# Attention with a quaternion map on one core: the program rewritten in steps of two heads, with row-tiled score pairs

## The reference

```
qkv  = x @ Wqkv.T + bqkv
attn = softmax(q @ k.T / 4)                     # per head, 512 x 512
coh  = sigmoid(tanh([x, cond] @ Wc1.T + bc1) @ Wc2.T + bc2)
mod  = attn * coh;  mod = mod / (mod.sum(-1) + 1e-8)
fa   = softmax(fp(cond) @ pe.T)                 # one row of 512 per sequence
out  = ((1 - 0.21) * mod + 0.21 * fa) @ v
x1   = x + out @ Wout.T + bout
y    = x1 + rotate(filter(x1))                  # one fixed linear map of the features
```

## Time and profile before

| | us |
|---|---|
| time, median of 3 runs | 379.8 |
| lowest and highest run | 374.76, 381.87 |
| span of the profiled execution, first to last instruction | 375.9 |
| TensorE busy | 321.0 (85%) |
| TensorE weight loads busy | 189.0 (50%) |
| VectorE busy | 223.9 (60%) |
| ScalarE busy | 176.9 (47%) |
| GpSimd busy | 156.8 (42%) |
| mean granted TensorE clock | 0.904 of 2.4 GHz |

### The profile page before, as it was taken

One profiled execution on the slowest core, in us unless ns is written; L12 is line 12 of the kernel. 1 busy time (PEld: TensorE's weight loads), 2 busy tenths in 40 slices (PEclk: granted clock), 3 DMA queues, 4 the chain that ended last, 5 costly groups with the idle time before them and its releaser, 6 DMA issues.

```text
span 375.9 us, 5338 instructions
## 1 busy us (share of the span) xinstructions
PE 321.0 (85%) x1537; PEld 189.0 (50%) x1537; DVE 223.9 (60%) x385; ACT 176.9 (47%) x323; POOL 156.8 (42%) x129
## 2 busy tenths in 40 slices
PE   0848849999799889999799689999799779999975
PEld 0634426555456456655456356655456346544423
DVE  3765943786568616687577407686577517775102
ACT  2101103765356625556456415565356525667750
POOL 9979950099991000299400000199500030296000
PEclk9986975999989958999899958999899969999996
DMA  8698498214953992216924991125943990200001
GB/s 245 247 125 99 146 127 123 83 58 99 125 59 112 126 163 51 75 66 127 124 30 145 149 118 36 62 78 112 118 51 122 124 146 1 84 1 2 1 1 57
DMA packets 16518, 35.87 MB, mean 95 GB/s; under 512 B 2724, under 2 KB 8228, under 8 KB 14456
## 3 DMA queue, kind: packets, MB, share of 16 engines
q1 hardware_dynamic: 14968, 34.47, 50.4%
q10 hardware_dynamic: 1536, 1.23, 1.2%
HBM read 25.07 MB, written 10.50 MB: 95 GB/s over the span
## 4 chain that ended last, share of the span: by engine, by line
PE 63%; DMA 24%; DVE 4%; ACT 3%; issue 3%; SPq 1%; ACTq 0%; DVEq 0%
PE smax_ps L996 14%; PE st_ps L1018 14%; PE o_ps L1030 13%; DMA stack<-max_rows 10%; DMA stack<-qk_scratch 10%; PE job_ps L894 9%; PE job_ps L929 3%; PE job_ps L970 3%; ACT probs L594 2%; DMA qk_scratch<-qk_lo 2%; PE job_ps L951 2%; DVE qk_lo L672 2%; PE smax_ps L982 2%; DMA w_raw<-wqkvT 1%; DVE maxima L746 1%
## 5 line engine op out<-in xcount | busy, mean ns | idle before, releaser
L746 DVE TENSOR_REDUCE maxima<-smax_ps 128x1 f32<-128x512 f32 x256 | 168.3, 686 | 113.6 <-PE smax_ps L996 113.0
L594 ACT ACTIVATE probs<-st_ps 128x512 f32<-128x512 f32 x247 | 142.6, 597 | 137.0 <-PE st_ps L1018 135.6
L996 PE MATMUL smax_ps<-stack 127*128 127x512 f32 x256 | 118.0, 464 | 13.8 <-DMA stack<-qk_scratch 11.9
L1018 PE MATMUL st_ps<-stack 128*128 128x512 f32 x247 | 107.7, 439 | 19.8 <-DMA stack<-max_rows 18.2
L996 PEld LDWEIGHTS smax_ps<-stack 127*128 127x128 f32 x256 | 52.0, 204 | 51.5 <-DVE maxima L746 24.4
L1030 PE MATMUL o_ps<-probs,vals 128*32 128x512 f32 x512 | 71.7, 634 | 1.0 <-ACT probs L594 0.9
L1018 PEld LDWEIGHTS st_ps<-stack 128*128 128x128 f32 x247 | 50.5, 205 | 39.6 <-DMA stack<-max_rows 19.8
L419 POOL TENSOR_TENSOR vals<-v_new,vals 128x256 f32<-128x256 f32 x16 | 10.0, 641 | 94.5 <-PE o_ps L1030 94.5
L401 POOL TENSOR_TENSOR x_lo<-x_raw,x_hi 128x1024 fp32r<-128x1024 f32 x3 | 7.2, 2388 | 65.7 <-ACT x_hi L550 65.7
L894 PE MATMUL job_ps<-x_hi,w_hi 128*128 128x512 f32 x48 | 22.0, 459 | 10.0 <-DVE w_lo L797 9.5
L519 POOL TENSOR_TENSOR prod<-amap,x_tok 128x1024 f32<-128x1024 f32 x12 | 28.6, 2383 | 0.9
(11 more groups left out here) (105 smaller groups left out, 305.5 us busy)
## 6 DMA issues: line engine op xcount, KB each, us to landing
stack<-qk_scratch SPq DMA_DIRECT2D x64, 256.0 KB, 9.7
qk_scratch<-qk_hi SPq DMA_DIRECT2D x16, 256.0 KB, 2.0
qk_scratch<-qk_lo SPq DMA_DIRECT2D x16, 256.0 KB, 2.0
x_tok<-x SPq DMA_DIRECT2D x4, 512.0 KB, 12.0
out<-y SPq DMA_DIRECT2D x8, 256.0 KB, 2.2
x_raw<-xT SPq DMA_DIRECT2D x3, 512.0 KB, 12.1
pe_tab<-fa_rows SPq DMA_DIRECT2D x4, 256.0 KB, 3.8
row<-rows SPq DMA_DIRECT2D x1, 936.0 KB, 7.6
```

Source lines behind the costliest of these rows:

```text
L594: nc.scalar.activation(probs[:, t % RING, :], st_bank(b, t)[:, :], ACT.Exp, scale=SCALE).then_inc(exp_done, 1)
L746: nc.vector.tensor_reduce(maxima[:, g % 2, n:n + 1], smax_ps[smax_bank(u)][:, :], AX_X, ALU.max).then_inc(smax_reduced, 1)
L996: nc.tensor.matmul(smax_ps[smax_bank(u)][:, :], stack[0:MAX_ROW, 0, h, i * P:(i + 1) * P], stack[0:MAX_ROW, 1, h, :], start=True, stop=Tru ...
L1018: nc.tensor.matmul(st_bank(b, t)[:, :], stack[:, 1, h, j * P:(j + 1) * P], stack[:, 0, h, :], start=True, stop=True).then_inc(st_filled, 1)
```

## The change

The program is written anew, unrolled over the batches, in 128 steps s of two heads (32 a batch, `PER`).

- **Paired score tiles.** The stack keeps three terms (48 rows) and the maximum's row, 49 rows, and holds two heads: one from partition 0, one from partition 64. A step's scores are two matrix products with operands at partitions 0 and 64, that is on the two halves of TensorE's rows, into two banks. The first pass works in such pairs too, 14 steps ahead (`LEAD`), with three banks for its pairs.
- **Exponentials over two banks.** One ScalarE instruction takes 128x1024 out of both banks (`exponentials`). There is one pair of banks; `scores(s)` waits for the exponential of s - 1. From step 116 (`WIDE`) a second pair is used, out of the first pass's banks. The ring holds 6 pairs, and `weigh_values` comes at even steps.
- **First group straight into the stack.** Group 0 of batch 0 is projected in fp32 with weights laid out in the stack's order (`direct`, two products of 512 columns for each of four tiles); ScalarE and VectorE write it into the stack (`direct_high`, `direct_low`). The first steps work through two pairs of the first pass each (`smax_at`).
- **Logits in column tiles.** `coherence_rows` uses the padded Wc2 as weights, 8 products in four column tiles, then one transposition ("zT").
- **Who does what.** ScalarE leaves one fp32 copy `qk_f` per projection, and GpSimd makes `qk_hi` and `qk_lo` of it (for batch 0 ScalarE writes the high part, too). A stack side goes out as 3 x 256 KB (the high part twice) and comes back in two DMAs of 384 KB a group. The maxima's DMAs (two for a group) are issued by SyncE, in one stream with the stack's reads, the stores and the loads. Projections are issued whole, at odd steps. x_hi, x_lo and y have two buffers. The map's table is made on 64 partitions and spread by TensorE. The output projection goes tile by tile.

The core of the diff:

```diff
-STEPS = G * IT * HG
-GS = IT * HG
-LEAD = 26
-RING = 8
-CUT = 16
...
+TERMS = 3
+MAX_ROW = TERMS * HD
+HALF = P // 2
+PAIRS = H // 2
+K_LO, Q_LO = 0, 2
...
+PER = G * IT * 2
+GS = IT * 2
+STEPS = B * PER
+RING = 6
 SMAX = 3
...
+def pair_of(s):
+    b, r = divmod(s, PER)
+    if s < GS:
+        return 0, 0, s % IT, s // IT
+    return b, r // GS, r % GS // 2, r % 2
...
+def av_step(n):
+    return 5 + n if n < IT else 2 * n + 2
...
+LEAD = 14
+AHEAD = IT
...
+def smax_at(s):
+    if s < LEAD - AHEAD:
+        return range(AHEAD + 2 * s, AHEAD + 2 * s + 2)
+    return range(s + LEAD, min(s + LEAD + 1, STEPS))
...
+JOB_STEP = {"q0": 3 - PER, "k0": 5 - PER, "q1": 17 - PER, "k1": 21 - PER, "v0": 23 - PER, "v1": 25 - PER,
+            "coh0": 29 - PER, "coh1": 31 - PER, "max0": -5, "max1": 3, "max2": 11, "max3": 19, "z": 7, "zT": 9,
+            "field": 13, "tokens0": 11, "tokens1": 19, "tokens2": 27, "tokens3": PER + 1, "back0": 22,
+            "back1": PER + 2, "out0": PER + 7, "out1": PER + 9, "out2": PER + 13, "out3": PER + 15}
+JOB_STEP_OF = {0: {"q0": -2, "k0": -2, "maxA": -1, "q1": 0, "k1": 1, "cond": 1, "maxB": 2, "v0": 2, "v1": 3,
+                   "coh0": 4, "coh1": 5, "max1": 6, "amap0": 6, "amap1": 7, "field_pre": 8, "z": 8, "zT": 9,
+                   "field_pair": 13, "field_logits": 15},
+               1: {"q0": 7 - PER, "k0": 9 - PER}}
...
+WIDE = STEPS - LEAD + 2
...
+            def write_hi(b, n, side):
+                if b:
+                    for g in (2 * n, 2 * n + 1):
+                        wait(sp, stack_loaded[g], 32 * (b if g else b - 1))
+                sp.wait_ge(qk_hi_done, 4 * b + 2 * n + side + 1)
+                dst = scratch[n, side].rearrange("t p s -> p t s")
+                dst = dst[:, 1:3] if side else dst[:, 0:2]
+                sp.dma_start(dst, qk_hi[:, side].bitcast(F32).unsqueeze(1).to_broadcast([P, 2, S])
+                             ).then_inc(qk_written, 16)
...
+            def read_stack(b, g):
+                wait(sp, st_filled, 2 * (PER * (b - 1) + GS * (g + 1)) if b else 0)
+                sp.wait_ge(qk_written, 64 * (2 * b + g // 2 + 1))
+                for a in range(2):
+                    first = g % 2 * HG + 2 * a
+                    src = scratch[g // 2].rearrange("a t (r h) s -> (t r) a h s", h=P // HD)
+                    sp.dma_start(stack[a * HALF:a * HALF + MAX_ROW, :, 2 * g:2 * g + 2, :].bitcast(F32),
+                                 src[:, :, first:first + 2, :]).then_inc(stack_loaded[g], 16)
+            def load_maxima(b, g, pp=None):
+                sp.wait_ge(max_rows_done, max_count(b, g) if pp is None else pp + 1)
+                if pp is None:
+                    wait(sp, stack_loaded[g], 32 * (b + 1 if g else b))
+                for a in range(2):
+                    at = a * HALF + MAX_ROW
+                    n = 2 * GS // 2 if pp is None else IT
+                    dst = stack[at:at + 1, 0, 2 * g:2 * g + 2, :] if pp is None else stack[at:at + 1, 0, pp:pp + 1, :]
+                    sp.dma_start(dst.bitcast(F32).rearrange("o h (i p) -> o (h i) p", p=P),
+                                 max_rows[a * n:(a + 1) * n, :].bitcast(F32)).then_inc(max_loaded, 16)
+            def load_field(b):
...
+            sp.wait_ge(dir_hi_done, 2)
...
+            load_x(1)
+            for side in range(2):
+                write_hi(0, 0, side)
+                write_lo(0, 0, side)
+            read_stack(0, 1)
+            load_maxima(0, 0, 0)
...
+            def qk_high(b, n, side):
+                pool.wait_ge(qk_f_done, 4 * b + 2 * n + side + 1)
+                pool.wait_ge(qk_written, 64 * (2 * b + n))
+                nc.gpsimd.tensor_copy(qk_hi[:, side, :], qk_f[:, side, :]).then_inc(qk_hi_done, 1)
+            def qk_low(b, n, side):
+                pool.wait_ge(qk_f_done, 4 * b + 2 * n + side + 1)
+                pool.wait_ge(qk_hi_done, 4 * b + 2 * n + side + 1)
+                wait(pool, qk_written, 64 * (2 * b + n))
+                nc.gpsimd.tensor_tensor(qk_lo[:, side, :], qk_f[:, side, :], qk_hi[:, side, :].bitcast(F32),
+                                        ALU.subtract).then_inc(qk_lo_done, 1)
...
+            def direct_high(pp, side):
+                act.wait_ge(dir_filled, 2 * pp + side + 1)
+                ps = (st_all[:, side], job_ps[side][:, :])[pp]
+                m = COL_DIRECT + 2 * pp + side
+                nc.scalar.activation(stack[:, side, pp, :], ps, ACT.Identity,
+                                     bias=col[:, m:m + 1]).then_inc(dir_hi_done, 1)
...
+            def exponentials(s):
+                act.wait_ge(st_filled, 2 * (s + 1))
+                if s >= RING:
+                    b, g, j, _ = pair_of(s - RING)
+                    act.wait_ge(av_done, IT * (G * b + g) + j + 1)
+                nc.scalar.activation(probs[:, s % RING].rearrange("p a s -> p (a s)"),
+                                     st_banks(s).rearrange("p a s -> p (a s)"), ACT.Exp,
                                      scale=SCALE).then_inc(exp_done, 1)
...
+            def direct_low(pp, side):
+                ps = (st_all[:, side], job_ps[side][:, :])[pp]
+                m = COL_DIRECT + 2 * pp + side
+                dve.wait_ge(dir_hi_done, 2 * pp + side + 1)
+                for a in range(2):
+                    at = a * HALF + (K_LO if side else Q_LO) * HD
+                    nc.vector.scalar_tensor_tensor(out=stack[at:at + HD, side, pp, :], in0=ps[at:at + HD, :],
+                                                   scalar=col[at:at + HD, m:m + 1],
+                                                   in1=stack[at:at + HD, side, pp, :].bitcast(F32),
...
+            def reduce_scores(u):
+                b, g, pp, i = smax_of(u)
+                for a in range(2):
+                    v = 2 * u + a
+                    at = (pp * 2 + a) * IT + i if b == 0 and g == 0 else (a * 2 + pp) * IT + i
+                    dve.wait_ge(smax_filled, 2 * u + 2)
+                    nc.vector.tensor_reduce(maxima[:, g % 2, at:at + 1], smax_all[:, v % SMAX], AX_X,
+                                            ALU.max).then_inc(smax_reduced, 1)
...
+            def direct(pp, side):
+                if side == 0:
+                    pe.wait_ge(ld_wdir[pp], 16)
+                ps = (st_all[:, side], job_ps[side][:, :])[pp]
+                c0 = (2 * pp + side) * P
+                for k in range(KT):
+                    ins = nc.tensor.matmul(ps, w_dir[:, k, c0:c0 + P], x_raw[:, k, :], start=(k == 0),
+                                           stop=(k == KT - 1))
+                ins.then_inc(dir_filled, 1)
...
+            def coherence_rows(b):
+                ps, done = claim("z", b)
+                pe.wait_ge(h_ready, KT * (b + 1))
+                if b == 0:
+                    pe.wait_ge(ld_wc2, 16)
+                for k in range(KT):
+                    for i in range(IT):
+                        ins = nc.tensor.matmul(ps[i * VW:(i + 1) * VW, 0:P], wc2[:, k, :], hT[:, k, i * P:(i + 1) * P],
                                                start=(k == 0), stop=(k == KT - 1))
...
+            def scores_for_max(u):
+                b, g, pp, i = smax_of(u)
+                if b == 0 and g == 0:
+                    pe.wait_ge(dir_lo_done, 4 * (pp + 1))
+                elif u % GS == 0:
+                    pe.wait_ge(stack_loaded[g], 32 * (b + 1 if g else b))
+                wait(pe, smax_reduced, 2 * u + 2 - SMAX)
+                for a in range(2):
+                    at = a * HALF
+                    nc.tensor.matmul(smax_all[:, (2 * u + a) % SMAX], stack[at:at + MAX_ROW, 0, 2 * g + pp, i * P:(i + 1) * P],
+                                     stack[at:at + MAX_ROW, 1, 2 * g + pp, :],
+                                     start=True, stop=True).then_inc(smax_filled, 1)
+            def scores(s):
+                b, g, j, pp = pair_of(s)
+                if s < GS:
+                    if j == 0:
+                        pe.wait_ge(max_loaded, 32 * (pp + 1))
+                        pe.wait_ge(ones_filled[pp], 32)
+                elif s % GS == 0:
+                    pe.wait_ge(max_loaded, 32 * max_count(b, g))
+                wait(pe, exp_done, st_before(s) + 1)
+                if s == WIDE + 1:
+                    pe.wait_ge(smax_reduced, 2 * STEPS)
+                banks = st_banks(s)
+                for a in range(2):
+                    at = a * HALF
+                    nc.tensor.matmul(banks[:, a], stack[at:at + MAX_ROW + 1, 1, 2 * g + pp, j * P:(j + 1) * P],
+                                     stack[at:at + MAX_ROW + 1, 0, 2 * g + pp, :],
...
+            pe.wait_ge(ld_x, 16)
+            direct(0, 0)
+            direct(0, 1)
+            scores_for_max(0)
+            direct(1, 0)
+            scores_for_max(1)
+            direct(1, 1)
+            scores_for_max(2)
+            project("q0", 0)
+            scores_for_max(3)
+            project("k0", 0)
+            maxima_rows("maxA", 0, 0)
```

(48 more changed lines are left out.)

1328 lines of the change are left out of this document (625 added, 703 removed).

## The result

| | before | after |
|---|---|---|
| median (lowest to highest) | 380.84 us (374.76 to 382.06) | 334.05 us (332.81 to 339.52) |
| ratio, 95% interval | 1 | 0.888 (0.876 to 0.900) |
| profiled execution: span | 375.9 us | 331.0 us (its time 333.57) |

The ratio and its interval, here and in the experiments, compare only executions that stayed out of a slower state in which some fall. The forecast was 326.0 us, from 303 to 367: the sign and the size hold, and the median lies 8 us above the forecast. That is not one small error: one stage took 22 us more than its term and the others 14 less, and that the two nearly cancel is luck.

What follows compares the result with a forecast made beforehand. TensorE's order was taken to bound the middle and a chain of transfers the setup; setup 41.5, batch 0 81.6, batches 1 and 2 67 each, batch 3 53, tail 12.6 make 322.7 us of span, 326 as time, range 303 to 367.

Steps and rivals of the forecast that it cites:

- The pair and the loop: Plain step: exponential 1.05, handovers 0.08 and pair of score products 0.61 make a loop of 1.74 us.
- The even step's 1.8: TensorE's stream in an even plain step: 0.04 + 0.46, second pair 0.23, change of tiles 0.1, values 0.99 us.
- Setup and its transfers: Before the first scores: a chain of projections, writes and reads, maxima queued behind group 1, ending at 41.5 us against 55.4.
- The stalls gone: Full batches: maxima arrive before they are wanted, so TensorE's 5.18 us stand and the low-clock stretches behind such stalls go.
- Batch 0: First batch 81.6 us: ten steps' reductions 24.6, VectorE jobs 5.6, 22 steps 38.9, jobs 5.5, stacks 3, clock 2, allowance 2.
- Rival 4: TensorE's clock falls to 1.2 GHz for good: 97 us a batch, 108 more in all, 434 us; chance 0.06.
- 1: Score pairs do not overlap: even step 2.26, odd 1.85, 367 us in all; chance 0.14.
- 2: Each change of TensorE's tile mode costs 0.27 instead of 0.1, some 60 a batch: 35 more, 361 us; chance 0.07.
- 3: Maxima queue behind the stack's reads, three groups a batch 3 us late: 25 to 30 more, 353 us; chance 0.11.
- batch 0 over 90: Condition for calling the forecast wrong: the first batch takes over 90 us, where 81.6 was forecast.
- the clock above 0.95: Sign that the forecast holds: TensorE's clock stays above 0.95.
- no idle time of TensorE over 2 us after step 10: Sign that the forecast holds: past the first ten steps TensorE never idles longer than 2 us.

Runs made afterwards that it cites:

- the alternating run: Changed kernel with, from step 10 on, each step's four products alternating between scores and first pass, so neighbours share row halves half and half: 361.53 us.
- the second experiment: Changed kernel with the load of the first maxima row issued ahead of the read of the stack's group 1: 327.78 us.
- the pairs of equal work above: Executions with the changed kernel's TensorE order in the first ten steps, which took 53.7 us at clock 0.75 down to 46.9: 45 us per unit of clock.
- experiment 4: Two separate edits of the changed kernel: a step's four products in alternating order, 361.53 us; each two-bank exponential split into two of 512 columns, 336.68 us.

## Why the prediction was right or wrong

**The pair and the loop: right.** Taken 0.61 from load to second end and 0.04 to hand over, measured 0.57 for both; exponential 1.05, measured 1.02. The odd step's loop of 1.74 is 1.64. The even step's 1.8 is 1.66: the second pair streams 0.34 after the first (165.05 to 165.39), where 0.46 was taken, and TensorE's own stream is thereby no longer than the loop. That is 0.1 a step, 3.4 a batch (56.5 - 32 x 1.66), and the allowance of 3.2 was not needed; the jobs came to 8.6 (61.76 - 32 x 1.66) against 7.6. Batches 1 and 2 were so 5.3 shorter each. The allowances of the sum add up to 9.9 (3.2 twice, 2 and 1.5), not to the 13 that the low end of the range takes off. The Trainium skill ("TensorE: Matmul & The Clock Gate", packing small matmuls) has tiles on different rows run together, and rows and the alternating run agree (0.50 for two). The Trainium skill ("TensorEngine Tiling (Array Packing)", key properties) has each change of mode drain the engine; TensorE busy 97% of a batch, with three modes in each two steps, and the step of 1.66 speak against a price that matters here.

**Setup and its transfers: right.** 41.5 for 39.73, by the same chain; the prediction named the queue that the second experiment then emptied.

**The stalls gone: right from batch 1 on.** In batches 1 to 3 no wait of TensorE's exceeds 1.0 us and the clock is 1.00.

**Batch 0: wrong, by 22.** The step that failed is "The first ten steps reduce 40 tiles: 24.6, and VectorE's jobs there 5.6". VectorE's sum was right (30.2 for 29.9 measured), but it was taken as the length of the stage, and TensorE's sum for the same steps was never made. From the pairs of equal work above, at a clock of 1.00 the ten would take 42.4 (46.9 - 0.10 x 45, an estimate), 32 of it TensorE's own stream and 9.6 waits for VectorE's first reduction; that is some 9 above the 33.2 that the prediction's terms for work and stacks make (24.6 + 5.6 + 3). The low clock adds 11.3, again by that estimate, where the prediction had 2: a projection took 2.86 at 0.50 (from 49.77) and 1.60 at 1.00 (from 150.44). Rival 4 thus came true in one stage, behind TensorE's wait of 12 us, and not in the steady part where it was feared. What keeps the clock low there after the wait was not separated. The rest, 3.5 in steps 10 to 31, is the hole at step 13 (8.7 above a plain step) less 5 that the other steps took under their 1.77, jobs and allowance. It was not in the sum: the prediction gave GpSimd the halves and did not follow what then stands behind them in GpSimd's stream, the power instruction, or runs beside them, VectorE's four small instructions.

**Rivals.** 1 did not occur; the alternating order of experiment 4 shows the part of it that comes of two products on the same half. 2 did not occur. 3 occurred once, at the setup and priced; made faster, batch 0 runs twice more into a transfer at the wrong place of the same queue. Of the prediction's two conditions for being wrong, "batch 0 over 90" came true (103.6), so by its own terms the forecast is wrong, however near the total. Of the other signs, the clock above 0.95 (0.927) and no idle time of TensorE over 2 us after step 10 (7.00) failed too, and the plain steps and full batches came out shorter than it said.

## What to carry to other kernels

Sum every stage for each engine, not only for the one that looks busiest, and ask where the engines wait for each other in turn: two sums of 30 and 32 gave 42. After a change that speeds the steady part, the first stage and the queue's order decide; each stall removed there moved to the next transfer in the same queue, until 2.3 us of it were left. And compare single executions by stage with the granted clock beside them: one order of work took 46.9 to 53.7 us for the same instructions.

## What the runs showed of the hardware that was not expected

- Four VectorE instructions on 4 partitions took 1.23 to 1.43 each beside GpSimd's products and 0.28 to 0.41 without: a duration in a profile is not that of an instruction alone. The Trainium skill ("SBUF — State Buffer", two separate sides) calls the port pair that VectorE shares with GpSimd an exclusive lock held for a whole instruction; both runs agree with it.
- 20 products that nobody reads, in a wait of 5.4, made the kernel 4.0 faster in the median (324.28 to 320.28).
- The tail's clock differs between runs: the same instructions from the last exponential to the end took 11.4 or 11.5 in five kernels, 12.9 in two and 13.7 to 14.2 in six, at mean clocks from 0.97 or more down to 0.61. The changed kernel's own executions differ by 7 us; how much of that is the tail was not measured.
- Two exponentials of 512 columns back to back need 1.09, not twice 0.597.
